# A recurrent encoder on one Trainium2 core: the conv band copied ahead of a row maximum, and a bias sum moved from VectorE to GpSimd

## The reference, cut to what matters

```
rp   = concat(region_tbl[region_idx], poi_tbl[poi_idx])
nv   = concat(rp @ W_rp + b_rp, coords @ W_co + b_co)
conv = elu(conv1d(nv, conv_w) + conv_b)                 # 8 steps
x    = concat(conv, broadcast(tanh(embeddings)))
h    = lstm(lstm(x, Wih0, Whh0), Wih1, Whh1)            # gates i, f, g, o
y    = ((h[:, -1] @ W1 + b1) @ W2 + b2) @ W3 + b3
```

## Time and profile before

| what | value |
|---|---|
| median of three runs | 1087.03 us |
| profiled execution | 1081.45 us |
| its span | 1079.6 us |
| PE, DVE, ACT, POOL busy | 1061.9, 741.5, 516.4, 328.7 us |
| share of the last chain on PE | 88% |
| mean granted TensorE clock | 0.996 of full |

### The profile page before, as it was taken

How to read it: one execution, slowest core, us unless ns; L and a number is a source line. 1 busy time by engine, 2 the same in 40 slices (tenths; PEclk the granted TensorE clock), 3 DMA queues, 4 the chain that set the end, 5 groups by cost and what they waited for, 6 DMA issues and landing times.

```text
span 1079.6 us, 14388 instructions
## 1 busy us (share of the span) xinstructions
PE 1061.9 (98%) x4905; PEld 508.5 (47%) x4905; DVE 741.5 (69%) x1155; ACT 516.4 (48%) x757; POOL 328.7 (30%) x353
## 2 busy tenths in 40 slices
PE   8899999999999999999999999999999999999998
PEld 7544444444445444444445444444444444444445
DVE  6688866765767766666867865567676775666554
ACT  3665344454555444434554544345554544444433
POOL 7660255625410065533440045552450000000000
PEclk9899999999999999999999999999999999999999
DMA  9410100000101100000101010000010110000001
GB/s 265 84 18 1 31 2 3 2 1 2 31 1 40 31 4 3 2 2 2 16 18 40 1 34 2 2 2 1 2 31 1 40 30 0 2 0 1 1 1 39
DMA packets 32082, 21.26 MB, mean 20 GB/s; under 512 B 19629, under 2 KB 25865, under 8 KB 32019
## 3 DMA queue, kind: packets, MB, share of 16 engines
q1 hardware_dynamic: 21223, 19.25, 6.2%
q0 software_dynamic: 9984, 1.12, 2.6%
q10 hardware_dynamic: 812, 0.07, 0.1%
HBM read 9.92 MB, written 4.19 MB: 13 GB/s over the span
## 4 chain that ended last, share of the span: by engine, by line
PE 88%; DVE 6%; issue 2%; ACT 2%; SPq 1%; DMA 1%; DVEq 0%; ACTq 0%
PE acc L1509 49%; PE acc L1500 27%; PE acc L1494 4%; PE aux L1731 2%; SPq L495 1%; PE aux L1422 1%; PE acc L1562 1%; PE acc L1571 1%; ACT gates L835 1%; DVE h_full L1188 1%; DVE gates L1141 1%; DVE h_part L1189 1%; ACT tanh_c L840 1%; PE aux L1461 1%; DMA w_nat<-in_L_rec_Wih 1%
## 5 line engine op out<-in xcount | busy, mean ns | idle before, releaser
L1509 PE MATMUL acc<-h_part,wh 128*128 128x512 f16 (+1 forms) x2640 | 644.2, 380 | 0.0
L1509 PEld LDWEIGHTS acc<-h_part,wh 128*128 128x128 f16 x2640 | 240.3, 98 | 314.2 <-issue 54.6
L1500 PE MATMUL acc<-h_part,wh 128*128 128x512 f16 (+1 forms) x1440 | 346.8, 379 | 0.0
L835 ACT ACTIVATE gates<-acc,gate_bias,unscale 128x512 f32<-128x512 f32 x246 | 189.8, 778 | 303.2 <-PE acc L1509 283.6
L835 ACT ACTIVATE gates<-gates,gate_bias,unscale 128x512 f32<-128x512 f32 x242 | 188.6, 810 | 141.6 <-DVE gates L1141 141.0
L1500 PEld LDWEIGHTS acc<-h_part,wh 128*128 128x128 f16 x1440 | 139.9, 98 | 171.4 <-issue 4.8
L652 POOL DMA_INDIRECT feat<-in_L_rec_region_tbl,region_idx x160 | 162.1, 1013 | 165.0 <-PE acc L1509 132.8
L1141 DVE TENSOR_TENSOR gates<-acc,emb_gates 128x512 f32<-128x512 f32 x242 | 160.2, 685 | 42.5 <-PE acc L1509 33.4
L652 POOL DMA_INDIRECT feat<-in_L_rec_poi_tbl,poi_idx x120 | 121.4, 1012 | 109.6 <-PE acc L1509 97.3
L1494 PE MATMUL acc<-x_in,wx 96*128 96x512 f32 (+1 forms) x242 | 134.8, 563 | 3.7 <-DVE gates L1141 2.5
L1188 DVE TENSOR_TENSOR h_full<-gates,tanh_c 128x512 f32<-128x512 f32 x120 | 82.7, 689 | 75.3 <-ACT tanh_c L840 75.3
(11 more groups left out here) (182 smaller groups left out, 418.6 us busy)
## 6 DMA issues: line engine op xcount, KB each, us to landing
out<-y SPq DMA_DIRECT2D x16, 256.0 KB, 2.1
x_in<-conv_hi SPq DMA_DIRECT2D x56, 64.0 KB, 2.0
feat<-in_L_rec_region_tbl,region_idx POOLq DMA_INDIRECT x160, 2.3
w<-in_L_rec_W SPq DMA_DIRECT2D x4, 512.0 KB, 6.4
w_nat<-in_L_rec_Whh SPq DMA_DIRECT2D x2, 1024.0 KB, 8.6
w<-in_L_rec_W SPq DMA_DIRECT2D x1, 2048.0 KB, 11.9
feat<-in_L_rec_poi_tbl,poi_idx POOLq DMA_INDIRECT x120, 2.3
x_in<-conv_lo SPq DMA_DIRECT2D x28, 64.0 KB, 2.0
```

The lines of the kernel that those rows point to most:

```text
L835: nc.scalar.activation(gates[layer][:, j, g, :], source, ACT.Tanh if g == GATE_G else ACT.Sigmoid, bias=gate_bias[:, layer, m:m + 1], scal ...
L1500: mm = nc.tensor.matmul(bank, wh[:, 1, a, c, rows], h_part[0][:, s.write_slot, b, c, :], start=(c == 0 and a == b == HI), stop=(s.first an ...
L1509: mm = nc.tensor.matmul(bank, wh[:, own_w, a, c, rows], h_part[layer][:, s.read_slot, b, c, :], start=False, stop=(c == HK - 1 and a == LO))
```

## The change

`put_band` and `put_conv_bias` move ahead of `row_maxima(2)`, and `put_wx_lo` moves ahead of `row_scales(1)`. The eight VectorE instructions of `head_sum` go. GpSimd gets `sum_head_bias` in their place, right after its last gather of batch 0: eight multiplications of a block of `w3` with its column of `b12`, in place, then seven additions into `head_sum`. It waits for the two head products (`head_acc`, 2), which read `w3`, and for `b12`. TensorE's product with the ones moves ahead of its fifth cell, and VectorE's addition of b3 ahead of VectorE's fifth cell. Each keeps its own wait: TensorE for the seventh addition, VectorE for TensorE's product.

```diff
--- before.py
+++ after.py
@@ -381,6 +381,7 @@
         w12_acc, w12_put = sem("w12_acc"), sem("w12_put")
         head_acc, head_hi_put, head_low_put = sem("head_acc"), sem("head_hi_put"), sem("head_low_put")
         b12_ready = sem("b12_ready")
+        head_sum_scaled = sem("head_sum_scaled")
         one_ready, head_sum_step, head_bias_acc, head_bias_put = (sem("one_ready"), sem("head_sum_step"),
                                                                   sem("head_bias_acc"), sem("head_bias_put"))
         coords_first_put = sem("coords_first_put")
@@ -638,6 +639,21 @@
                                                 poi_part[:, k, :], ALU.subtract).then_inc(poi_part_step, 1)
                         pool.wait_ge(poi_part_step, k + 1)
 
+            def sum_head_bias():
+
+                pool.wait_ge(head_acc, 2)
+                pool.wait_ge(b12_ready, 1)
+                for k in range(K2):
+                    nc.gpsimd.tensor_scalar(w3[:, k, :], w3[:, k, :], b12[:, k:k + 1], None, ALU.mult
+                                            ).then_inc(head_sum_scaled, 1)
+                pool.wait_ge(head_sum_scaled, 2)
+                nc.gpsimd.tensor_tensor(head_sum[:, :], w3[:, 0, :], w3[:, 1, :], ALU.add).then_inc(head_sum_step, 1)
+                for k in range(2, K2):
+                    pool.wait_ge(head_sum_scaled, k + 1)
+                    pool.wait_ge(head_sum_step, k - 1)
+                    nc.gpsimd.tensor_tensor(head_sum[:, :], head_sum[:, :], w3[:, k, :], ALU.add
+                                            ).then_inc(head_sum_step, 1)
+
             for n in range(NB):
                 tiles = None
 
@@ -703,6 +719,7 @@
                         landed = rows_in[0 if t < WIN else 1]
                         gather_steps(t, t + 1, False, landed)
                         pool.wait_ge(landed, (t - (PAIR_WIN if t < WIN else WIN) + 1) * GR * DMA)
+                    sum_head_bias()
                 else:
 
                     for c in range(CH):
@@ -1040,17 +1057,6 @@
                 dve.wait_ge(b2_put, 1)
                 nc.vector.tensor_tensor(b12[:, :], w12_t[:, :, H], b2_col[:, :], ALU.add).then_inc(b12_ready, 1)
 
-            def sum_head_bias():
-
-                dve.wait_ge(w3_in, DMA)
-                dve.wait_ge(b12_ready, 1)
-                nc.vector.tensor_scalar(head_sum[:, :], w3[:, 0, :], b12[:, 0:1], None, ALU.mult
-                                        ).then_inc(head_sum_step, 1)
-                for k in range(1, K2):
-                    dve.wait_ge(head_sum_step, k)
-                    nc.vector.scalar_tensor_tensor(head_sum[:, :], w3[:, k, :], b12[:, k:k + 1], head_sum[:, :],
-                                                   ALU.mult, ALU.add).then_inc(head_sum_step, 1)
-
             def put_head_lo(a):
                 dve.wait_ge(head_hi_put, a + 1)
                 nc.vector.tensor_tensor(w_head[:, LO, a, :], head_bank, w_head[:, HI, a, :].bitcast(F32),
@@ -1267,11 +1273,11 @@
             poi_one_hot(3, POI_PIECES)
             row_maxima(1)
             put_poi()
-            row_maxima(2)
             put_band()
             put_conv_bias()
+            row_maxima(2)
+            put_wx_lo()
             row_scales(1)
-            put_wx_lo()
             put_wh_lo(0)
             add_biases()
             elu(0, slice(0, HALF), (0, slice(0, HALF)), ())
@@ -1297,14 +1303,13 @@
             indices(1, "region", REG, later, (later_idx_in, 2 * DMA))
             cell(third)
             cell(fourth)
-            sum_head_bias()
             dve.wait_ge(idx_ready, 2)
             indices(2, "poi", POI, later, (later_idx_in, 2 * DMA))
             elu(chunk_of(0, 1), slice(0, NCOL), (1, slice(0, NCOL)), [])
-            cell(fifth)
             dve.wait_ge(head_bias_acc, 1)
             dve.wait_ge(b3_in, DMA)
             nc.vector.tensor_tensor(b_head[:, :], aux[:, 0, :], b3_row[:, :], ALU.add).then_inc(head_bias_put, 1)
+            cell(fifth)
 
             for stage in stages(dve, NB, STEPS):
                 kind = stage[0]
@@ -1426,7 +1431,7 @@
 
             def sum_head_bias():
                 pe.wait_ge(one_ready, 1)
-                pe.wait_ge(head_sum_step, K2)
+                pe.wait_ge(head_sum_step, K2 - 1)
                 nc.tensor.matmul(aux[:, 0, :], one_col[:, 0:1].to_broadcast([P, P]), head_sum[:, :], start=True,
                                  stop=True).then_inc(head_bias_acc, 1)
 
```

## The result

The changed kernel takes 1095.34 us (median of 22 runs, 1089.23 to 1099.34) against 1090.24 for the kernel before, run beside it (22 runs, 1086.06 to 1091.85): 5.1 us more. The ratio is 1.0049, 95% interval 1.0034 to 1.0064. The forecast was +4.1 us and 1091.1, range 1085 to 1097; of the 4.2 us between 1091.1 and 1095.34, 3.2 are the kernel before, whose median of 22 runs is 1090.24 and not the 1087.03 of the first three. The changed kernel's profiled execution took 1097.22 us (span 1095.4).

What follows compares the result with a forecast made beforehand. TensorE was taken as the bound, busy 1061.9 of 1079.6 us. The terms 0 (band) - 2.1 (late waits gone) + 6.2 (turn-taking) gave +4.1 us, 1087.0 + 4.1 = 1091.1 us, with a range of 1085 to 1097.

Steps and rivals of the forecast that it cites:

- Part 1: Set-up: band copy ahead of third maxima starts line 1359 1.6 us earlier, but TensorE still waits until 34.66: 0.
- Part 2: Fourth cell to sixth cell's end: sum off VectorE removes TensorE's late waits at 122.39 and 129.97, gaining 2.1 us.
- Part 3: GpSimd's sum undisturbed: multiplications 0.70 each, additions 1.50, ending at 100.7, stalling TensorE's product with the ones 0.7 us.
- The nearest row by number of inputs: GpSimd's multiplication priced at 0.70 us from one-input copies, since it too has one tensor input.
- Part 4: Third and fourth cells: GpSimd and VectorE take turns on two-SBUF-input instructions, making VectorE's first fourth-cell sum 6.2 us late.
- GpSimd's duration less 0.1: Price of each put-off VectorE instruction in the third-cell stretch: 0.6 us for a multiplication, 1.4 for an addition.
- rival B: Before the fifth cell: GpSimd slower than thought, or idle TensorE loses its clock; 1095.0 us (1093 to 1098), chance 0.27.
- Rival A: Fourth cell: no real GpSimd-VectorE disturbance, first sum stays at 92.2; -1.4 us, 1085.6 (1084.9 to 1086.3), chance 0.22.
- Rival C: Set-up: band move shifts the slow-clock stretch at 34.4 to where TensorE has little to do; up to -3.3 us, chance 0.06.

Runs made afterwards that it cites:

- e1_band: Kernel before plus only the band part (band and conv bias ahead of the third maxima, weights' low parts ahead of the scales): 1091.84 us, ratio 0.9998.
- e3_no_sum: Changed kernel with GpSimd's multiplications and additions left out, TensorE's product reading the first block of w3: 1089.13 us, ratio 0.9975 to the kernel before.
- e7_immediate: Changed kernel with GpSimd's eight multiplications by an immediate constant instead of the b12 column: 1097.58 us in one run, kernel before 1093.27.
- e5_write_only: Changed kernel without the band part, GpSimd's fifteen instructions replaced by seven that only write, sum left out: 1089.90 us in one run, kernel before 1093.27.
- e6_late: Changed kernel without the band part, GpSimd's sum begun after VectorE's fourth-cell sums, product and b3 behind the fifth cell: 1096.87 us, kernel before 1093.27.

## Why the prediction was right, and where it was not

- Part 1 (the band) at 0: right in size, ratio 0.9998 in e1_band, but not shown in its mechanism. The forecast let the band copy free line 1359 1.6 us early and the wait for the gathered rows swallow that. In every later profile, with the band part or without, that product starts after a wait of only 0.27 or 0.28 us, at 29.1 to 32.2 (30.93 in the change; forecast 26.1), because TensorE's own work before it ends late; the 1.89 of the earlier trace rows, which the part was to save, is in the first profile alone. The feature transposes (1440, 1435 before) came at 35.61, near the 34.66 of the earlier trace rows, and a wait of 6.28 stood behind them, before 42.49. Why the set-up takes 10 us more in all these profiles than in the first is open. They share one thing that the first lacks: between 15 and 50 us ScalarE waits 10 to 16 us in all with the label "remote" in the profile (12.5 in the change). No run was made for it.
- Part 2, a gain of 2.1: measured 2.4 by e3_no_sum (stretch), 2.7 by its ratio, and 2.3 between the conv product and the sixth cell's end in the change.
- Part 3, GpSimd alone. The multiplication was the mis-sized term: 0.70 forecast from the copies, 1.57 measured, a little beyond the upper end of 1.50. e7_immediate shows that the column is not to blame. "The nearest row by number of inputs" was the wrong choice. The additions came out near the forecast (1.50; 1.53 measured, a start every 1.68 at the most), in part by luck: without waiting they take 1.26 or 1.27, and the rest is the turn-taking, which the forecast put on top.
- Part 4, the turn-taking: right in kind, and the lateness of the first sum, forecast 6.2, was 6.6. The number agrees by luck, since its terms do not. Forecast were seven multiplications at 0.6, two additions at 1.4 and 0.8 hidden in VectorE's waits. Measured were four put-offs by multiplications of 0.21 to 0.42 (1.4 in all), six by additions, five of 0.87 to 1.07 and one of 0.22 (5.2 in all), and nothing hidden. So the additions did most of it. "GpSimd's duration less 0.1" is near for an addition with its own 1.27 (it loses the rest of it less 0.14) and far too dear for a multiplication. That six additions and not two met VectorE there I put down to two things: multiplications twice as long, and the late set-up, which moves VectorE by 9.9 us and GpSimd not at all (its sum starts at 83.56; forecast 83.8). With the set-up of the first profile, GpSimd's end at 109.8 would have been the bound, well behind TensorE's 106; that is argued, and there is no profile of the changed kernel in that state.
- The sum left out the clock on the forecast's side: rival B put "up to 3.3" on it; it came to 1.8 (tile pitch and windows above). Forecast 4.1; profile 6.1; medians 5.1.
- Rival A (no disturbance) fell by VectorE's lengths; its place and its deciding point, the first sum, were the right ones to watch. Rival B's two conditions both came true, multiplications of 1.5 us and a clock that falls behind TensorE's wait, and the measured 1095.3 is its 1095.0 rather than the forecast's 1089.5 to 1092.5; but 3.2 of the 4.2 us above the forecast are the kernel before, dearer than its first three runs said, and the +10 to +11 us that B gave for such multiplications did not come, because each put VectorE off by 0.42 at the most. Of the difference itself, +5.1 lies inside the forecast's +2.5 to +5.4. Rival C did not come about (e1_band).
- The rule of the Trainium skill that I weighed (SBUF — State Buffer, "SBUF: two separate sides") goes further than my forecast did: it limits the two-input case to a GpSimd instruction that reads SBUF, and it includes VectorE instructions in a two-port mode against any. e5_write_only agrees with the first half (0.68 and 0.69 stayed); line 953 growing from 0.22 to 1.47 would fit the second, but no run shows in which mode it ran. The rule lets the engine that came second wait for the whole instruction of the other. The additions agree with it to 0.14 us; the multiplications do not, since the VectorE instructions that they lengthened ended 0.33 us before them.

## What to carry to other kernels

Work moved from VectorE to GpSimd need not leave VectorE freer while both read SBUF: here 5.9 us taken from its queue came back as 6.6 us of lateness, at a place with no slack. Before moving work to another engine, look for the waits in the queue that has it: three of eight instructions put into waits of 0.77 us gave nearly all that removing the sum could give. And compare two profiles from a common point inside the program, not by their spans; here two thirds of the difference of spans was the set-up of one execution.

## What the runs showed of the hardware that was not expected

- GpSimd's 128x512 multiplication by a scalar takes 1.48 us (a constant) to 1.57 us (a column), more than its two-input addition when that has not had to wait (1.26 or 1.27), while its copy of 128x384 takes 0.51.
- A VectorE instruction with two SBUF inputs that met a GpSimd addition ended 0.54 to 0.56 us after the addition, in six cases of six in the change; one that a multiplication lengthened ended 0.33 or 0.34 before it, in four of four.
- GpSimd's memsets did not lengthen VectorE's two-input instructions (0.68 and 0.69 in nine cases), but did hold up a one-input one from SBUF to SBUF (0.22 to 1.47), as an addition did in e7_immediate (0.22 to 1.31).
- A wait of TensorE of 5.9 us was followed by tiles at half the clock (2.82 us for the first, about 1.54 usual), as was one of 5.7 us in e6_late, where the product with the ones took 2.04 instead of 1.02.
